# A gated-delta-rule layer with its feed-forward gate: earlier weight loads and deeper buffers ahead of the recurrent part, and another order of calls inside it

## What is computed

```python
xn = layernorm(x)
# attention branch: 32 value heads, 16 key heads, head size 128
mixed = silu(conv4(xn @ W_qkv)); q, k, v = split(mixed)
beta, g = sigmoid(xn @ W_b), -exp(A_log) * softplus(xn @ W_a + dt_bias)
q, k = l2norm(q) * 128 ** -0.5, l2norm(k)
for t in range(512):                      # the recurrence, per head
    S = S * exp(g[t])
    S = S + beta[t] * outer(k[t], v[t] - k[t] @ S)
    o[t] = q[t] @ S
s = (rmsnorm(o) * norm_w * silu(xn @ W_z)) @ W_out
# gate branch: 8 experts (top 2) of width 176, one shared of width 704
hid = silu(xn @ W_gate) * (xn @ W_up) * scale(token, expert)
g = silu(hid @ W_down)
out = x + s * g
```

## Time and profile before

| | |
|---|---|
| median of 3 runs | 2868.14 us (2868.12 to 2871.74) |
| the profiled execution | 2867.33 us, its span 2865.6 us |
| TensorE matmul busy | 2636.6 us, 92% of the span; 34,330 matmul passes and as many weight loads |
| VectorE, ScalarE, GpSimd busy | 2002.9, 1621.1, 1074.0 us |
| mean granted TensorE clock | 0.982 of full |
| prepare_block, ffn_block, recurrent_block begin at | 0, about 102, about 500 us |

### The profile page before, as it was taken

How to read it: one execution, slowest core, us unless ns; L and a number is a source line. 1 busy time by engine, 2 the same in 40 slices (tenths; PEclk the granted TensorE clock), 3 DMA queues, 4 the chain that set the end, 5 groups by cost and what they waited for, 6 DMA issues and landing times.

```text
span 2865.6 us, 88023 instructions
## 1 busy us (share of the span) xinstructions
PE 2636.6 (92%) x34330; PEld 1955.6 (68%) x34330; DVE 2002.9 (70%) x4880; ACT 1621.1 (57%) x5068; POOL 1074.0 (37%) x1391
## 2 busy tenths in 40 slices
PE   3299999799999999999999999999999999999995
PEld 2155665577777777777777777777777777777774
DVE  3233222788888888778877888788878887788773
ACT  2111111566666666666666666666666666666662
POOL 0210220444444444444444444444444444444440
PEclk9799999899999999999999999999999999999997
DMA  1511220211121211111111111111111111111111
GB/s 43 164 39 24 62 62 1 73 42 57 42 57 42 57 49 49 49 49 49 49 49 49 49 49 49 49 49 49 49 49 49 49 49 49 49 49 49 49 49 62
DMA packets 225647, 146.87 MB, mean 51 GB/s; under 512 B 187457, under 2 KB 195937, under 8 KB 225121
## 3 DMA queue, kind: packets, MB, share of 16 engines
q1 hardware_dynamic: 219104, 123.58, 15.0%
q0 software_dynamic: 6144, 17.83, 2.6%
HBM read 115.81 MB, written 2.70 MB: 41 GB/s over the span
## 4 chain that ended last, share of the span: by engine, by line
PE 63%; DVE 9%; ACT 3%; issue 2%; DMA 2%; SPq 1%; POOL 1%; DVEq 0%; POOLq 0%; ACTq 0%
PE rps L811 11%; PE rps L736 8%; PE rps L744 7%; DVE conv L1264 6%; PE rps L698 4%; PE rps L828 4%; PE rps L715 3%; PE rps L867 3%; PE rps L858 3%; PE rps L682 3%; PE rps L841 3%; PE rps L776 2%; PE rps L785 2%; PE rps L708 2%; PE rps L685 2%
## 5 line engine op out<-in xcount | busy, mean ns | idle before, releaser
L1264 DVE SCALAR_TENSOR_TENSOR conv<-rps,w_in,conv 128x509 f32<-128x509 f32 (+2 forms) x768 | 571.9, 745 | 65.7 <-ACT conv L1052 47.6
L811 PE MATMUL rps<-xnT,w_in 128*128 128x512 f32 x1024 | 505.1, 616 | 13.5 <-DVE cols L1246 13.5
L1463 POOL TENSOR_TENSOR decay_b<-decay,beta_k 128x512 f32<-128x512 f32 x128 | 130.4, 1040 | 486.5 <-DVE beta_k L1280 486.5
L744 PE MATMUL rps<-w_z,xnT 128*128 128x256 f32 x1040 | 275.2, 388 | 0.9 <-ACT z L1001 0.7
L811 PEld LDWEIGHTS rps<-xnT,w_in 128*128 128x128 f32 x1024 | 174.7, 190 | 147.3 <-issue 123.9
L1414 POOL TENSOR_TENSOR o_t<-o_sq,q_mean 128x8 f32<-128x8 f32 x65 | 13.2, 204 | 688.6 <-ACT gated L985 688.6
L1052 ACT ACTIVATE conv<-rps,w_in 128x512 f32<-128x512 f32 x256 | 175.9, 687 | 163.2 <-PE rps L811 160.3
L736 PE MATMUL rps<-w_outn,gatedT 128*128 128x256 f32 x1056 | 241.4, 381 | 1.1 <-ACT gatedT L995 0.7
L441 DVE TENSOR_TENSOR silu_g<-fps_u,silu_g 128x512 f32<-128x512 f32 x68 | 47.0, 691 | 277.5 <-PE fps_u L460 127.7
L736 PEld LDWEIGHTS rps<-w_outn,gatedT 128*128 128x128 f32 x1056 | 201.7, 191 | 49.7 <-issue 23.8
L1066 ACT ACTIVATE qkT<-conv 128x512 f32<-128x512 f32 x128 | 80.6, 629 | 220.7 <-DVE conv L1264 220.7
(11 more groups left out here) (216 smaller groups left out, 6483.0 us busy)
## 6 DMA issues: line engine op xcount, KB each, us to landing
sums_row<-g_rows SPq DMA_DIRECT2D x65, 1024.0 KB, 5.0
scale<-comb_rows POOLq DMA_DIRECT2D x40, 256.0 KB, 5.4
w_in<-in_w_in SPq DMA_DIRECT2D x17, 520.0 KB, 3.5
bq<-bmat SPq DMA_DIRECT2D x256, 32.0 KB, 2.0
inv<-xq SPq DMA_DIRECT2D x256, 32.0 KB, 1.9
w_z<-in_w_z SPq DMA_DIRECT2D x17, 256.0 KB, 2.6
w_out<-in_w_out SPq DMA_DIRECT2D x17, 256.0 KB, 5.0
invT<-xqT SPq DMA_DIRECT2D x128, 32.0 KB, 2.1
```

Source lines behind the costliest of these rows:

```text
L744: last = nc.tensor.matmul(ps[Z_BANK[c // 2]][:, (c % 2) * D:(c % 2 + 1) * D], xnT[:, m, tb * T + c * C:tb * T + (c + 1) * C], w_z[:, m, :] ...
L811: last = nc.tensor.matmul(ps[PROJ_BANK[j]][:, :], w_in[:, m * 4 * P + j * P:m * 4 * P + (j + 1) * P], xnT[:, m, b * T:(b + 1) * T], start= ...
L1264: nc.vector.scalar_tensor_tensor(conv[:, j, shift:T], ps[PROJ_BANK[j]][:, 0:T - shift], w_in[:, k:k + 1], conv[:, j, shift:T], ALU.mult, A ...
L1463: nc.gpsimd.tensor_tensor(decay_b[:, us, :], decay[:, us, :], beta_k2[:, us].unsqueeze(2).to_broadcast([P, NC_, C]), ALU.mult).then_inc(db ...
```

## The change

Ahead of the recurrent part: `xn` and the PSUM tiles of the loop over 16 tiles are four deep instead of two, ScalarE copies the transpose once, the small projection reads `xnT`, and all loops over sequences in the first two blocks are unrolled. The 9 weight transfers of the feed-forward part move from ffn_block's start to prepare_block's first transfers, and TensorE's first wait asks only for constants and small weights. For the first sequence, `scale` is waited for at column tile 8 (`LATE`) instead of 0: products go to `hid` unscaled, and from tile 8 on VectorE scales two of them after each product. Inside the recurrent part the same calls stand in another order, on TensorE, ScalarE, VectorE and GpSimd; no call is added or removed.

```diff
 KINDS = 7
+DEEP = 4
+LATE = FT // 2
...
-        xn = sb("xn", [P, 2, D])
-        xt = sb("xt", [P, 2, D])
+        xn = sb("xn", [P, DEEP, D])
...
-            sp.dma_start(cst[:, :], keep["cst_dram"]).then_inc(w_loaded, 16)
-            sp.dma_start(ws[:, :, :], small_w).then_inc(w_loaded, 16)
+            sp.dma_start(cst[:, :], keep["cst_dram"]).then_inc(c_loaded, 16)
+            sp.dma_start(ws[:, :, :], small_w).then_inc(c_loaded, 16)
             sp.dma_start(dtb[:, :], decay_rows[0:1, :].partition_broadcast(P)).then_inc(w_loaded, 16)
             sp.dma_start(a_exp[:, :], decay_rows[1:2, :].partition_broadcast(P)).then_inc(w_loaded, 16)
+
+            for k, (j0, j1) in enumerate(GROUPS):
+                part = slice(j0 * P, j1 * P)
+                sp.dma_start(ffn["wg"][:, :, part], ffn["wg_dram"][:, :, part]).then_inc(ffn["w_in"][k], 16)
+                sp.dma_start(ffn["wu"][:, :, part], ffn["wu_dram"][:, :, part]).then_inc(ffn["w_in"][k], 16)
+            sp.dma_start(ffn["wd"][:, :, :], ffn["wd_dram"]).then_inc(ffn["wd_in"], 16)
...
+            def normalise(t):
+
+                if t >= DEEP:
+                    dve.wait_ge(xnt_ps, t - DEEP + 1)
+                nc.vector.tensor_scalar(xn[:, t % DEEP, :], xs[:, t, :], mean[:, t:t + 1], rstd[:, t:t + 1],
+                                        ALU.subtract, ALU.mult).then_inc(xn_ready, 1)
+
+            def take_small(t):
+                b, c, k = t // NC_, t % NC_, t % DEEP
+
+                dve.wait_ge(small_ps, t + 1)
+                nc.vector.tensor_copy(a_bv[:, :, b:b + 1, :, c],
+                                      ps_s[k][:, 0:NV].rearrange("p (h o v) -> p h o v", v=REP, o=1)).then_inc(small_out, 1)
+                nc.vector.tensor_copy(a_av[:, :, b:b + 1, :, c],
+                                      ps_s[k][:, NV:2 * NV].rearrange("p (h o v) -> p h o v", v=REP, o=1)).then_inc(small_out, 1)
+                nc.vector.tensor_copy(routed[:, t:t + 1, :], ps_s[k][:, 2 * NV:NSMALL]).then_inc(small_out, 1)
+
+            for t in range(TILES + DEEP - 1):
+                if t < TILES:
+                    normalise(t)
+                if t >= DEEP - 1:
+                    take_small(t - DEEP + 1)
...
-            act.sem_inc(xt_kept, BASE)
-            with act.Fori(0, BATCH) as b:
-                for c in range(NC_):
-                    k = c % 2
-                    act.wait_ge(xnt_ps, b * NC_ + c + 1 + BASE)
-
-                    act.wait_ge(small_ps, b * NC_ + max(c - 1, 0) + BASE)
-                    nc.scalar.activation(xt[:, k, :], ps_t[k][:, 0:D], ACT.Copy).then_inc(xt_ready, 1)
-                    nc.scalar.activation(xnT[:, :, bass.ds((b * NC_ + c) * P, P)],
-                                         ps_t[k][:, 0:D].rearrange("p (k t) -> p k t", k=KT), ACT.Copy).then_inc(xt_kept, 1)
+            for t in range(TILES):
+                act.wait_ge(xnt_ps, t + 1)
+                nc.scalar.activation(xnT[:, :, t * P:(t + 1) * P],
+                                     ps_t[t % DEEP][:, 0:D].rearrange("p (k t) -> p k t", k=KT), ACT.Copy).then_inc(xt_kept, 1)
...
+            pe.wait_ge(c_loaded, 32)
+
+            def transpose_tile(t):
+                pe.wait_ge(xn_ready, t + 1)
+                if t >= DEEP:
+                    pe.wait_ge(xt_kept, t - DEEP + 1)
+                for m in range(KT):
+                    last = nc.tensor.transpose(ps_t[t % DEEP][:, m * P:(m + 1) * P], xn[:, t % DEEP, m * P:(m + 1) * P], ident)
+                last.then_inc(xnt_ps, 1)
+
+            def project_small(t):
+                pe.wait_ge(xt_kept, t + 1)
+                if t >= DEEP:
+                    pe.wait_ge(small_out, TILES + 3 * (t - DEEP + 1))
+                for m in range(KT):
+                    last = nc.tensor.matmul(ps_s[t % DEEP][:, 0:NSMALL], xnT[:, m, t * P:(t + 1) * P], ws[:, m, :],
+                                            start=(m == 0), stop=(m == KT - 1))
+                last.then_inc(small_ps, 1)
+
+            for t in range(TILES + 1):
+                if t < TILES:
+                    transpose_tile(t)
+                if t:
+                    project_small(t - 1)
...
-            with pool.Fori(0, BATCH) as b:
+            for b in range(BATCH):
...
-                    act.wait_ge(hid_done, b * FT + max(j - 1, 0) + BASE)
+                    act.wait_ge(prod_done if b == 0 else hid_done, b * FT + max(j - 1, 0) + BASE)
...
+                def scaled(j):
+                    dve.wait_ge(prod_done, b * FT + j + 1 + BASE)
+                    src = hid[:, j, :] if b == 0 else silu_g[:, j % 2, :]
+                    nc.vector.tensor_tensor(hid[:, j, :], src, scale[:, j, :], ALU.mult).then_inc(hid_done, 1)
+
+                if b:
+                    dve.wait_ge(scale_in, (b + 1) * 16 * len(spans))
                 for j in range(FT):
                     dve.wait_ge(silu_done, b * FT + j + 1 + BASE)
                     dve.wait_ge(u_ps, b * FT + j + 1)
                     if j == 0:
 
                         dve.wait_ge(o_ps, b * NC_ + BASE)
-                    nc.vector.tensor_tensor(silu_g[:, j % 2, :], ps_u[j % 2][:, :], silu_g[:, j % 2, :],
-                                            ALU.mult).then_inc(prod_done, 1)
-                    dve.wait_ge(prod_done, b * FT + j + 1 + BASE)
-                    nc.vector.tensor_tensor(hid[:, j, :], silu_g[:, j % 2, :], scale[:, j, :],
-                                            ALU.mult).then_inc(hid_done, 1)
+                    dst = hid[:, j, :] if b == 0 else silu_g[:, j % 2, :]
+                    nc.vector.tensor_tensor(dst, ps_u[j % 2][:, :], silu_g[:, j % 2, :], ALU.mult).then_inc(prod_done, 1)
+                    if b:
+                        scaled(j)
+                    elif j >= LATE:
+                        if j == LATE:
+                            dve.wait_ge(scale_in, 16 * len(spans))
+                        for q in (2 * (j - LATE), 2 * (j - LATE) + 1):
+                            if q < FT:
+                                scaled(q)
...
                     join_w(n)
+                    project(0)
                     join_x(n)
-                    project(0)
+                    halves_w(n)
                     by_token(1)
-                    halves_w(n)
+                    halves_x(n, r)
                     project(2)
-                    halves_x(n, r)
-                    gated_transpose(n, 0)
-                    k_products(1)
                     pe.wait_ge(v_done, n(2))
                     solve(0)
-                    project(3)
+                    k_products(1)
                     attend(0)
+                    gated_transpose(n, 0)
                     pe.wait_ge(tap_done, n(12) + 6)
                     gated_transpose(n, 1)
                     read_state(1)
+                    project(3)
+                    solve(1)
+                    k_products(0)
+                    pe.wait_ge(ksq_done, n(1) + 1)
+                    pe.wait_ge(kw_done, n(2) + 2)
+                    project_out(n, 0, loads)
+                    attend(1)
                     by_token(0)
-                    solve(1)
-                    by_token(2)
-                    k_products(0)
-                    attend(1)
+                    read_state(2)
+                    project_out(n, 1, loads)
+                    solve(2)
+                    spread_rows()
+                    pe.wait_ge(qsq_done, n(1) + 1)
+                    project_out(n, 2, loads)
                     pe.wait_ge(wz_in, (i + (1 if b == 0 else 2)) * 16)
                     pe.wait_ge(tap_done, n(12) + 12)
                     project_z(tb, 0)
-                    read_state(2)
+                    project_out(n, 3, loads)
                     project_z(tb, 1)
-                    solve(2)
-                    spread_rows()
-                    pe.wait_ge(ksq_done, n(1) + 1)
-                    pe.wait_ge(kw_done, n(2) + 2)
-                    project_out(n, 0, loads)
-                    project_out(n, 1, loads)
-                    pe.wait_ge(qsq_done, n(1) + 1)
-                    project_out(n, 2, loads)
-                    project_out(n, 3, loads)
+                    by_token(2)
                     attend(2)
+                    pe.wait_ge(acc_done, n(2) + 1)
+                    project_z(tb, 2)
                     merge_w(0)
                     read_state(3)
                     merge_x(0)
                     solve(3)
-                    pe.wait_ge(acc_done, n(2) + 1)
-                    project_z(tb, 2)
+                    project_z(tb, 3)
+                    merge_w(1)
+                    by_token(3)
                     attend(3)
-                    by_token(3)
-                    merge_w(1)
-                    project_z(tb, 3)
                     merge_x(1)
...
+                    if b == 2:
+                        act.wait_ge(out_ps, n(2))
+                        scale_out_weights(i + 2)
                     take_join(n)
```

(25 more changed lines are left out.)

133 lines of the change are left out of this document (45 added, 88 removed).

## The result

The changed kernel takes 2836.58 us (median of 7 runs, 2823.50 to 2853.03) beside 2867.85 us (7 runs, 2865.28 to 2871.74) for the kernel before: a ratio of 0.989, 95% interval 0.987 to 0.992. The profiled execution is the median one, with a span of 2834.7 us. The changed kernel's runs spread over 29.5 us where those before spread over 6.5, which is a first hint that something in it happens by chance. The mean granted TensorE clock goes with it: 0.971 of full in the fastest of the seven, 0.962 in the slowest; in the kernel before it is 0.981 to 0.983.

What follows compares the result with a forecast made beforehand. TensorE's matmuls were taken to bound the recurrent part, with removable waits ahead of it. 2867.3 - 55 + 0 + 16 + 10 = 2838, and 0.8 for the median gave 2839 us; range 2806 to 2869.

Steps and rivals of the forecast that it cites:

- loop over tiles: Start of the kernel: four buffers and one ScalarE copy let VectorE start L209 at 48, not 67.74; gain 20 us.
- weights: Feed-forward block: weights loaded during prepare_block no longer hold up its first matmul; gain 4.3 us.
- scales and cold restart: Feed-forward block: TensorE's 29.1 us wait for the scales and 1.9 us of slow passes after it both go.
- ahead of the recurrent part: Everything before the 64 steps: gains of 20, 4.3, 29.1 and 1.9 sum to 55 us, between 47 and 61.
- first calls and rest of the order: Recurrent steps: 0.75 us of waiting against 0.83, nothing gained; 0 taken, bounds -6 and +32 us.
- late transfer: At halves_w, now ready earlier, SyncE's second L657 transfer lands too late: 0.25 us a step, 16 us more.
- instruction supply: At merge_x, blocks of 256 instructions arrive late with thinner cover: 10 us more, bounds 0 and 26.
- recurrent part: The 64 steps: order 0, transfer 16 and instruction blocks 10, a cost of 26 us.
- rival E: TensorE falls to the lower clock level in part of each step, 120 us more: 2960 us; chance 0.02.
- Rival B: Recurrent order worth something: transfer hidden, supply gaps don't grow, waits close further; 2787 to 2813 us; chance 0.14.
- C: Late instruction blocks become the bound of the merges in the recurrent steps: 2919 us, slower; chance 0.11.

Runs made afterwards that it cites:

- e1: The change in prepare_block and ffn_block alone, with the recurrent part's order as in the kernel before: 2798.91 us, ratio 0.976.
- e2: Only the new order inside the recurrent part, with everything ahead of it as in the kernel before: 2899.18 us, ratio 1.011.
- h3: f1 with project_z(tb, 2) put behind the first merge_w of a step: 2791.51 us, ratio 0.975.
- e4: The changed kernel with eight useless transposes added between join_x and halves_w: 2809.91 us, ratio 0.980.
- f1: The changed kernel with project(2) in two calls, its first matmul moved between join_x and halves_w: 2779.35 us, ratio 0.968.
- h2: The changed kernel with a step's first eight TensorE calls as in the kernel before: 2874.12 us, ratio 1.003.
- e3: The changed kernel with one useless matmul added between join_x and halves_w: 2813.21 us, ratio 0.982.
- g1: e1 with two pairs of banks instead of four in the loop over tiles: 2822.75 us, ratio 0.984.

## Why the prediction was right, and where it was wrong

The forecast of 2839 us stands 2.4 from the median, and that it stands so near is luck: ahead of the recurrent part it missed 11 us of gain, inside it 8.6 us of loss, and the two met. Of its marks, steps of 36.0 us (36.14), the gaps before `join_x` gone and "issue" gaps under 60 us came; the first feed-forward matmul near 82 us came at 71.89, L209's work at 37.62 and not 48, the first `project_out` at 473.71 and not near 490, and of the 62 gaps before `halves_w` 22 ended with transfers.

| step of the prediction | forecast, us | measured, us |
|---|---|---|
| loop over tiles | -20 (-16 to -25) | -30.05 |
| weights | -4.3 | -4.8 |
| scales and cold restart | -31.0 | -31.2 |
| ahead of the recurrent part | -55 (-47 to -61) | -66.05 |
| first calls and rest of the order | 0 (-6 to +32) | -15 |
| late transfer | +16 (0 to +23) | +8, in the line of the first calls |
| instruction supply | +10 (0 to +26) | +4 beside before, 0 beside e1, in the same line |
| clock | only as rival E, +120 | +50 |
| recurrent part | +26 | +34.6 |

**The loop** was mis-sized. Its start came earlier than I had it (the first transposes at 22.66, and the table load at 0.74, no longer ahead of the copies), its period at the lower level was 1.19 us and not 1.40, and the clock rose at 29.5. I had that rise as the lower bound, and ruled it out for the main value with no row that spoke against it.

**Weights and scales** came as worked out: from L344 to the first product 20.52 us before and 15.72 after, and from there to the recurrent part 31.2 us less. The scales were in before the ninth tile needed them; VectorE never waited.

**The first calls** were walked rightly: `halves_w` waits 0.54 us (I had 0.55), `halves_x` starts at +7.50 (7.5), and an undisturbed step takes 34.7 us, 0.15 under the earlier trace rows. The conclusion from it, that 0.75 us of waiting against 0.83 gives nothing, holds for undisturbed steps. 0.15 us in 62 steps are 9 us. The 5.9 us in 16 waits of L698 for `resid` are gone from the waits view besides, which the prediction put at nothing: together the 15 us.

**The late transfer** was there, and cost half of its price. The waits view names VectorE's copies (L1220) for all 60 waits at `halves_w`, but where the wait is long the copy had long been done. One such wait: timeline of TensorE, timeline of VectorE, and the landing times of the two L655 transfers (L657 before), issued at 932.54 and 933.20:

```profile
936.86 0.53 PE L774 MATMUL rps<-invT,bmat 64*64 64x64 f32 x6 [1.49 <-DVE inv L1220]
935.42 0.42 DVE L1220 COPY invT<-rps 32x256 f32<-32x256 f32 x1 [0.15 <-PE rps L765]
DMA to landing us min/median/max: 1.9/2.7/3.6
```

`invT` was ready at 935.84, the second transfer landed at 936.77, and `halves_w` began 0.09 us later. Beside the landing times 22 of the 62 waits end so, 0.09 us behind the last landing; they are 19.6 us in all, 8.0 more than 22 of 0.53 us. Of these 22 steps 12 fall, of the other 40 11, so the late transfer seems to bear on the clock too. I had priced a landing time spread evenly from 1.9 to 4.0 us, and taken 0.25 us a step of it; 0.13 came.

**Instruction supply** takes 25.4 us of gaps in the changed kernel, 21.8 in the kernel before, 25.5 in e1, which has the order of before, and 29.1 in e2, which has only the new one. So the term of 10 us came as about 4, and e1, whose cover is that of before, is as far from 21.8; h3's thicker cover made the step no shorter either. The Trainium skill (Runtime: NRT & Kernel Launch, "Instruction fetch mechanics") has fetching as mostly hidden. The trace agrees as far as 31 gaps for 256 blocks are "mostly", and it shows that bursts of 128 instructions in 0.7 us are where it is not hidden, in gaps of up to 1.3 us at `merge_x`.

**Rival E** is the step that failed: I gave it 0.02 because "no gap in my walk is over 0.8 us". The gap in the walk was 0.55 us, and waits of 0.53 us and more were followed by a fall in 22 of 62 steps. The mechanism was E's, but not its size (a fall in a third of the steps, about 2 us each, and not one in all), and not its cause: I had transposes and small tiles in mind, and e4 shows that transposes side by side with them hold the clock. The chance should have been that of a mechanism for which the trace of before has no case, rather than of one excluded.

**Rival B** has its part too: without the falls the changed kernel would have taken about 2837 - 50 = 2787 us, rival B's number and outside my range, and f1, which lacks the falls and the late transfer's waits, took 2779. The chances had a slip as well: C and E are both slower, 0.13 together, where I wrote 0.11.

## To carry to other kernels

Where TensorE is the bound and waits a little, look at what stands around the wait: 0.5 us with full-size projections one call away on both sides cost 0.5 us, and the same 0.5 us in the middle of a longer run of small calls went with a fall of the clock, about 2 us, in every third step. Such a loss shows in the granted clock and in longer passes, in no wait; a useless filler in the empty place is the cheap test for it, and half of a divisible call, put there, is the cure. When calls are moved on one engine, walk the queues of the engines that feed it as well, since two of my variants lost 75 and 198 us because calls of TensorE had moved and ScalarE's copies for them had not.

## What the runs showed of the hardware

- A granted clock of 0.50 for 3.4 or 6.8 us follows waits of 0.53 to 1.49 us in a run of small calls (22 of 62 steps), and not waits of 0.48 to 1.04 and 0.82 us that have full-size projections between them (h2, 0 of 62).
- Eight transposes of 128 x 128 held the clock as well as a matmul of 128 x 512: no fall in either (e3, e4).
- The clock rose to its upper level within a loop of two transposes and four passes of 73 columns a tile once nothing in it waited (0.96 to 0.56 or 0.67 us), and stayed low with a wait of 0.78 us a tile (0.97, g1).
- A wait that a trace names after an engine can be another's: 22 waits of `halves_w` ended 0.09 us after a transfer had landed, under the name of a VectorE copy that had been done for up to 0.9 us.
- Times spread more with falls (29.5 us over 7 runs of the changed kernel, whose granted clock goes from 0.971 to 0.962 with it, and 3.8 us over 4 of e1), but that isn't all: e3 and f1, with none and one, spread over 15 and 16 us.
